# Two stages re-ordered: gathered rows turned inside the second product, and an attention stage with its sums at the head of the step

## The chip, the cores and the metric

The kernel runs on one core of a Trainium2 chip. A core has TensorE (PE in the profile, its weight loads PEld), VectorE (DVE), ScalarE (ACT), GpSimd (POOL) and SyncE (SP), which here only issues transfers. The metric is device time in microseconds (us) of one execution; the median of three runs of the kernel before is 3226.8 us.

## The reference

The input x has 8 sequences of 512 tokens with 256 features. Six residual stages follow each other, each on a layer norm of x:

```python
x = x + 0.5 * L0_ffn(ln(x))    # 64 experts, top 3, capacity 128
x = x + L0_attn(ln(x))
x = x + 0.5 * L0_ffn(ln(x))
x = x + 0.5 * L1_ffn(ln(x))    # 8 experts, top 2, dense
x = x + L1_attn(ln(x))
x = x + 0.5 * L1_ffn(ln(x))
```

The change touches the first two kinds. `L0_ffn` gathers 128 rows for each expert, and computes `gelu(buf @ w1 + b1) @ w2 + b2` (256 to 1024 to 256), scales by the gate and adds the rows back. `L0_attn` is a windowed attention, 16 heads of 16, where each token looks at itself and 31 before it:

```python
strain = disp_win - disp[:, :, :, None, :]
state = masked mean of (strain @ w_state + b_state) over the window
bond_act = gelu(strain @ w_strain + b_strain + state @ w_state_i + state_win @ w_state_j + rel_emb @ w_pos)
damage_act = gelu(strain @ w_damage + b_damage)
logits = bond_act @ w_bond_out + b_bond_out - 10 * sigmoid(damage_act @ w_damage_out + b_damage_out)
out = softmax(masked logits) applied to val_win, then @ w_cproj + b_cproj
```

## The kernel before, in words

The whole of x stays in SBUF (`core.tile`). The stages run one after another, each in a block of its own, in which every engine has a program of its own, written out in order; semaphores join them. An engine that waits holds back all that stands behind it. All of the products named here are in float32, which TensorE does in two passes.

**Sparse stage** (`experts`, twice). Per expert e TensorE runs `up(e + 1)`, `turn_rows(e + 2)`, `down(e)`. `turn_rows` (L1621) transposes the 128 gathered rows in two pieces into one PSUM bank, which VectorE copies to `rows_t` (L1686); `up` (L1633) is the first product, 16 matmuls; `down` (L1644) is the second, 8 matmuls, which accumulate in another bank. GpSimd adds expert e's result back to memory (L1593), for which it waits until the one before has landed, then gathers the rows of expert e + 4 (L1583), all with four buffers. SyncE loads the 2 MB of weights of expert e + 4 when expert e is done.

**First attention** (`attn0_phase`, once). The work of one sequence (a batch) is 16 steps of four relative places for eight heads. In step s:

- GpSimd writes damage chunk s + 1 (L2041), VectorE bond chunk s + 1 (L2373), each into a ring of three buffers;
- ScalarE applies GELU to bond and damage chunk s (L2304, L2309), and after every fourth step a tanh to the group's damage sums (L2317);
- TensorE reduces both chunks of step s - 1 with `columns` (L2088), at the end of its step. Before it in the step stand the other pieces: turning a group's logits, the finishing of one tile of the previous batch's output, spread over four steps (`turn_weights`, `sums`, `turn_ctx`, `project`), and the token products of the next chunks: `make_q`, `make_a`, `make_c`, `values`, tokens and means. The constants `A1_Q, C1_Q, Q1_Q, V_Q, XN_Q, XM_Q, Q0_Q, A0_Q, C0_Q` say in which of the 16 steps each stands.

When a batch's logits are complete, VectorE finds the top of each row (`find_top`, L2407), GpSimd subtracts it (`less_top`, L2048), ScalarE takes exponentials (L2323), and SyncE stores the weights in memory in slanted rows of 128 bytes (`skew_weights`, four stores and one load for a batch), which gives them back shifted to the window. Tile m starts its finishing at step 13 + 4 (m + 4), and waits for the addition of tile m - 1. After the last chunk (step 128) seven tiles, 25 to 31, are left. `softmax_batch` has no upper bound, so a ninth softmax runs in these steps, on data that nobody reads.

## Time and profile before

| | |
|---|---|
| runs | 3226.8, 3223.7, 3229.19 us |
| profiled execution | 3219.98 us, span 3218.2 us |
| busy share of the span | PE 90%, DVE 51%, ACT 47%, POOL 42% |
| mean granted TensorE clock | 0.947 |
| sparse stages, steady part | 159.31 to 612.58 and 1535.97 to 1990.11 us |
| first attention, first to last GELU | 684.65 to 1313.9 us |
| its tail | to 1398.8 us |

The page's busy shares are averages over six stages. Which engine is full in one stage, and which waits, has to be read from windows of that stage. In a row of the timeline the bracket at the end is the idle time of that engine ahead of the row and what ended it. The transfers are issued by SyncE's queue (SPq); the length of such a row is that of the issue, not of the transfer.

### The profile page before, as it was taken

The page shows a single profiled execution, that of the slowest core. Times are in us where ns is not written, and L with a number is a line of the kernel's source. Part 1 is how long each engine was busy: PE and PEld are TensorE (multiplying, and loading weights), DVE is VectorE, ACT ScalarE, POOL GpSimd, SP SyncE. Part 2 cuts the span into 40 slices and gives each one's busy share as a digit, 9 for nine tenths or more (in the row PEclk, how much of TensorE's full clock was granted, in tenths as well). Part 3 has the DMA queues.
Part 4 walks back from the last instruction along what each step waited for, and adds up shares of the span by engine and source line. Part 5 has one row for each costly group of instructions (what it writes and reads, how often), then busy time and mean ns, then how long its engine had stood idle before and what let it go on. Part 6 is the DMA issues. An engine that isn't in the chain of part 4 may idle for free. (4 is left out here: it accounts for less than half of the span.)

```text
span 3218.2 us, 53908 instructions
## 1 busy us (share of the span) xinstructions
PE 2896.9 (90%) x19497; PEld 2067.5 (64%) x19497; DVE 1649.1 (51%) x4513; ACT 1527.6 (47%) x2577; POOL 1346.6 (42%) x1333
## 2 busy tenths in 40 slices
PE   5899999768999999568999999899969999998999
PEld 4799999733444443247999998566635666655666
DVE  4411111168888888455111111566676666665666
ACT  1133333249988888410333332233347777772332
POOL 3444444359989888335344443000043344320000
PEclk9899999989999999757999999899989999998999
DMA  7199999713544444641899997200052233301000
GB/s 278 40 302 317 321 316 319 239 30 20 61 60 60 59 59 60 94 168 53 262 319 321 322 313 236 82 0 0 8 142 72 70 88 95 95 2 37 13 13 20
DMA packets 354987, 431.81 MB, mean 134 GB/s; under 512 B 84528, under 2 KB 312771, under 8 KB 350659
## 3 DMA queue, kind: packets, MB, share of 16 engines
q1 hardware_dynamic: 330178, 395.16, 44.2%
q0 software_dynamic: 24576, 33.57, 4.8%
q8 instruction: 144, 2.36, 0.3%
q14 instruction: 89, 0.72, 0.1%
HBM read 355.80 MB, written 72.88 MB: 133 GB/s over the span
## 5 line engine op out<-in xcount | busy, mean ns | idle before, releaser
L1674 ACT ACTIVATE f_h_t<-f_h_ps,f_b_t 128x128 f32<-128x128 f32 x1024 | 320.4, 364 | 617.1 <-PE f_h_ps L1633 617.1
L2041 POOL TENSOR_TENSOR a_dmg_buf<-a_c 128x2048 f32<-128x2048 f32 x128 | 520.1, 4096 | 65.6 <-PE a_dmg_ps L2088 43.9
L1633 PEld LDWEIGHTS f_h_ps<-f_rows_t,f_w 128*128 128x128 f32 x4096 | 481.5, 193 | 9.9 <-issue 3.5
L1633 PE MATMUL f_h_ps<-f_rows_t,f_w 128*128 128x128 f32 x4096 | 482.6, 276 | 2.3 <-DVE f_rows_t L1686 1.2
L1644 PE MATMUL f_y_ps<-f_w,f_h_t 128*128 128x256 f32 x2048 | 462.9, 379 | 0.0
L1593 POOL DMA_INDIRECT acc_rows<-f_y,f_give x128 | 205.0, 1602 | 509.1 <-DMA acc_rows<-f_y,f_give 372.1
L1644 PEld LDWEIGHTS f_y_ps<-f_w,f_h_t 128*128 128x128 f32 x2048 | 379.3, 190 | 46.4
L2373 DVE SCALAR_TENSOR_TENSOR a_bond_buf<-a_a,a_small_rep,a_q_ps 128x512 f32<-128x512 f32 x512 | 346.9, 741 | 36.8 <-PE a_bond_ps L2088 35.1
L428 DVE SCALAR_TENSOR_TENSOR x_resid<-f_y_ps,f_gate,x_resid 128x256 f32 x512 | 218.7, 479 | 162.5 <-PE f_y_ps L311 156.9
L885 ACT ACTIVATE a_prob<-a_prob,a_neg_top 128x384 f32<-128x384 f32 (+3 forms) x512 | 276.5, 570 | 47.3 <-POOL a_neg_top L702 46.9
L299 PE MATMUL f_h_ps<-f_xn_t,f_w 128*128 128x512 f32 x584 | 282.5, 611 | 3.3 <-DVE f_xn_t L176 1.8
L998 DVE CUSTOM_DVE_ANT_0 a_prob<-a_s_ps,a_factor 128x384 f32<-128x384 f32 (+3 forms) x512 | 234.4, 486 | 86.5 <-PE a_s_ps L779 84.5
L360 ACT ACTIVATE f_h_t<-f_h_ps,f_b 128x512 f32<-128x512 f32 x146 | 100.3, 687 | 368.6 <-PE f_h_ps L299 368.3
L311 PEld LDWEIGHTS f_y_ps<-f_w,f_h_t 128*128 128x128 f32 x1152 | 219.6, 191 | 86.2 <-issue 55.1
L311 PE MATMUL f_y_ps<-f_w,f_h_t 128*128 128x256 f32 x1152 | 270.5, 380 | 0.1
L1686 DVE COPY f_rows_t<-f_t_ps 128x256 f32<-128x256 f32 x128 | 54.4, 425 | 408.4 <-PE f_t_ps L1621 408.4
L2309 ACT ACTIVATE a_dmg_buf<-a_dmg_buf,a_small_rep 128x2048 f32<-128x2048 f32 x128 | 255.2, 1994 | 4.9 <-POOL a_dmg_buf L2041 4.8
L2304 ACT ACTIVATE a_bond_buf<-a_bond_buf,a_bond_act_b 128x2048 f32<-128x2048 f32 x128 | 255.5, 1996 | 2.0 <-DVE a_bond_buf L2373 1.8
L1693 DVE TENSOR_TENSOR f_y_biased<-f_y_ps,f_b 128x256 f32<-128x256 f32 x128 | 54.4, 425 | 393.4 <-PE f_y_ps L1644 381.3
L790 PE MATMUL a_t_ps<-ident,a_prob 128*128 128x128 f32 x1280 | 231.1, 280 | 17.6 <-ACT a_prob_t L896 13.5
L896 ACT COPY a_prob_t<-a_t_ps 128x512 f32<-128x512 f32 (+1 forms) x352 | 192.8, 548 | 100.7 <-PE a_t_ps L790 99.5
L702 POOL TENSOR_SCALAR a_neg_top<-a_top 128x1 f32<-128x1 f32 x512 | 105.1, 209 | 323.5 <-DVE a_top L998 298.5
(333 smaller groups left out, 4274.5 us busy)
## 6 DMA issues: line engine op xcount, KB each, us to landing
f_w<-in_L_ffn_w_dram SPq DMA_DIRECT2D x256, 1024.0 KB
a_skewed<-skew SPq DMA_DIRECT2D x8, 2048.0 KB, 8.4
a_k_s<-parts SPq DMA_DIRECT2D x16, 768.0 KB, 7.8
acc_rows<-x_resid SPq DMA_DIRECT2D x17, 512.0 KB, 4.5
xn_rows<-f_xn SPq DMA_DIRECT2D x16, 512.0 KB, 3.0
x_resid<-acc_rows SPq DMA_DIRECT2D x16, 512.0 KB, 7.5
a_vals<-val_rows SPq DMA_DIRECT2D x64, 128.0 KB, 5.3
skew<-a_bond SPq DMA_DIRECT2D x32, 256.0 KB
```

The lines of the kernel that those rows point to most:

```text
L299: last = nc.tensor.matmul(h_ps[(k * NE + n) % 2][:, :], w1_sb[:, RUN[n], c, :], norm.xn_t[k][:, c, :], start=c == 0, stop=c == DC - 1)
L311: last = nc.tensor.matmul(y_ps[m % YB][:, j, :], h[:, t * P:(t + 1) * P], w2_sb[:, RUN[n], :], start=True, stop=True)
L790: last = nc.tensor.transpose(t_ps[pack % TB][:, col + kb * P:col + (kb + 1) * P], prob[:, u % PR, kb * P:(kb + 1) * P], core.ident[:, :])
L885: nc.scalar.activation(prob[:, u % PR, 0:width], prob[:, u % PR, 0:width], ACT.Exp, bias=neg_top[:, u % PR:u % PR + 1]).then_inc(exp_ready, 1)
L998: nc.vector.tensor_tensor_reduce(out=prob[:, u % PR, 0:width], in0=s_ps[use % SB][:, 0:width], in1=factor[:, S - width:S], scale=1.0, scal ...
L1633: last = nc.tensor.matmul(h_ps[n // HB][:, (n % HB) * P:(n % HB + 1) * P], w1_sb[s][:, c, n * P:(n + 1) * P], rows_t[e % 2][:, c, :], star ...
L1644: last = nc.tensor.matmul(y_ps[k][:, 0:D], h_t[k][:, n, :], w2_sb[e % R][:, n, :], start=n == 0, stop=n == HC - 1)
L1674: nc.scalar.activation(h_t[k][:, n, :], h_ps[n // HB][:, (n % HB) * P:(n % HB + 1) * P], ACT.Gelu, bias=b1_t[:, n, e:e + 1]).then_inc(gelu ...
L2041: nc.gpsimd.tensor_tensor(dmg_buf[n % RING][:, :, :], places(c_sb[h], first_place(dg)), c_sb[h][:, PAD:].unsqueeze(1).broadcast_to([P, DG, ...
L2304: nc.scalar.activation(buf[:, :, :], buf[:, :, :], ACT.Gelu, bias=bond_act_b[:, h:h + 1]).then_inc(bond_act, 1)
L2309: nc.scalar.activation(buf[:, :, :], buf[:, :, :], ACT.Gelu, bias=small_rep[:, B_DAMAGE:B_DAMAGE + 1]).then_inc(dmg_act, 1)
L2373: last = nc.vector.scalar_tensor_tensor(out=bond_buf[n % RING][:, dd, :], in0=a_sb[h][:, d + 1:d + 1 + S], scalar=small_rep[:, POS + d:POS ...
```

## The change

- `down` turns the rows of expert e + 2 between its fourth and its fifth matmul.
- In the attention stage TensorE's step starts with `columns`. `make_q` and `make_a` are cut into a beginning and an end, in two steps, and the constants spread the pieces over the batch. VectorE copies what step s - 1 made at the head of step s, right behind its chunk.
- The first normalisation is VectorE's instead of GpSimd's; the later ones stand one chunk earlier.
- The bias of the output projection is split into three bf16 rows, so its product is one bf16 matmul instead of two float32 passes.
- The stores and loads of the weights go by tile, sixteen and four of them instead of four and one. For the last batch top, subtraction and exponential go by tile too.
- From tile 26 on (`LATE`) tiles start two steps apart and use banks that are free by then, so that they overlap.
- The ninth softmax is gone.

```diff
                 for n in range(HC):
+                    if n == HC // 2 and e + 2 < E:
+                        turn_rows(e + 2)
                     pe.wait_ge(gelu_done, e * HC + n + 1)
                     last = nc.tensor.matmul(y_ps[k][:, 0:D], h_t[k][:, n, :], w2_sb[e % R][:, n, :],
                                             start=n == 0, stop=n == HC - 1)
...
             for e in range(E):
                 if e + 1 < E:
                     up(e + 1)
-                if e + 2 < E:
-                    turn_rows(e + 2)
                 down(e)
 
         @block.scalar
...
-    LAST = CHUNKS + FIRST + TPB * FIN
+    LATE = FINISHES - TPB - 2
+    LATE_FIN = 2
     NTP = 8
     XN, XM, A0, C0, A1, C1 = 0, 2, 4, 5, 6, 7
-    V_Q = (3, 7)
-    XN_Q, XM_Q, Q0_Q, A0_Q, C0_Q = 7, 9, 11, 12, 13
-    A1_Q, C1_Q, Q1_Q = 1, 2, 3
...
+        second = lambda m: dmg_ps if m >= LATE else o_ps
+        ctx_bank = lambda m: bond_ps[1][:, 0:D] if m >= LATE else o_ps[:, D:2 * D]
+        project_bank = lambda m: bond_ps[0] if m >= LATE else o_ps
...
+        def begin(m):
+            return FIRST + (m + TPB) * FIN if m <= LATE else begin(LATE) + (m - LATE) * LATE_FIN
+        FINISH_AT = {begin(m): m for m in range(FINISHES)}
+        LAST = begin(FINISHES - 1) + FIN
...
-            x, now = divmod(s - FIRST, FIN)
-            return x - TPB if s >= FIRST and now == stage else None
...
-            return i - 1 if now == q and i > 0 else None
+            return i - 1 if now == q and 0 < i <= B else None
+        def soft_parts(j):
+            return [slice(x, x + 1) for x in range(TPB)] if j == B - 1 else [slice(0, TPB)]
...
-                sp.wait_ge(exp_done, j + 1)
-                if j:
-                    sp.wait_ge(skew_loaded, j * 16)
-                for a in range(BPT):
-                    row = TPB * NH * SPAN
-                    rows = bass.AP(tensor=skew_dram.tensor, offset=a * WIN * row + 1,
-                                   ap=[[row + 1, WIN], [SPAN, TPB * NH], [1, WIN]])
-                    sp.dma_start(rows, bond[j % 2][a * WIN:(a + 1) * WIN, :, :, :].rearrange(
-                        "p j h w -> p (j h) w")).then_inc(skew_stored, 16)
-                if j:
-                    sp.wait_ge(w_turned, j * TPB)
-                sp.wait_ge(skew_stored, (j + 1) * 16 * BPT)
-                sp.dma_start(skewed[:, :, :].rearrange("p j s -> p (j s)"), skew_dram).then_inc(skew_loaded, 16)
+                row = TPB * NH * SPAN
+                for x in range(TPB):
+                    if x < len(soft_parts(j)):
+                        sp.wait_ge(exp_done, j + x + 1)
+                    if j:
+                        sp.wait_ge(skew_loaded[x], j * 16)
+                    for a in range(BPT):
+                        rows = bass.AP(tensor=skew_dram.tensor, offset=a * WIN * row + x * NH * SPAN + 1,
+                                       ap=[[row + 1, WIN], [SPAN, NH], [1, WIN]])
+                        sp.dma_start(rows, bond[j % 2][a * WIN:(a + 1) * WIN, x, :, :]).then_inc(skew_stored[x], 16)
+                for x in range(TPB):
+                    if j:
+                        sp.wait_ge(w_turned, (j - 1) * TPB + x + 1)
+                    sp.wait_ge(skew_stored[x], (j + 1) * 16 * BPT)
+                    sp.dma_start(skewed[:, x, :], skew_dram[:, x * NH * SPAN:(x + 1) * NH * SPAN]
...
-            normalise(0)
+                for n, tiles in enumerate(soft_parts(j)):
+                    count = tiles.stop - tiles.start
+                    rows = bond[j % 2][:, tiles, :, :].rearrange("p j h w -> p (j h) w")
+                    pool.wait_ge(top_ready, j + n + 1)
+                    nc.gpsimd.tensor_tensor(rows, rows, top[:, tiles.start * NH:tiles.stop * NH, :].broadcast_to([P, count * NH, WIN]),
+                                            ALU.subtract).then_inc(soft_ready, 1)
...
 
             def turn_weights(m):
                 j, x = divmod(m, TPB)
-                if x == 0:
-                    pe.wait_ge(skew_loaded, (j + 1) * 16)
-                before = values_before(FIRST + (m + TPB) * FIN)
...
                 if before:
                     pe.wait_ge(val_copied, before)
-                if m:
+                if m > LATE:
+                    pe.wait_ge(w_copied_act, m)
+                    pe.wait_ge(w_copied_dve, m)
+                elif m == LATE:
+                    pe.wait_ge(tanh_done, ALL_GROUPS)
...
                     pe.wait_ge(proj_added, m)
                 for hp in range(HP):
...
+                if m == LATE:
+                    pe.wait_ge(proj_added, m)
+                if m > LATE:
+                    pe.wait_ge(ctx_ready, m)
...
             def turn_ctx(m):
                 pe.wait_ge(ctx_ready, m + 1)
+                if m == LATE:
+                    pe.wait_ge(logits_copied, ALL_GROUPS)
...
+                if m == 0:
+                    pe.wait_ge(b_out_split, 1)
+                if m > LATE:
+                    pe.wait_ge(proj_added, m)
                 for c in range(DC):
-                    nc.tensor.matmul(o_ps[:, 0:D], ctx_t[:, c, :], w_out_sb[:, c, :], start=c == 0, stop=False)
...
+                    nc.tensor.matmul(project_bank(m)[:, 0:D], ctx_t[:, c, :], w_out_sb[:, c, :], start=c == 0, stop=False)
+                nc.tensor.matmul(project_bank(m)[:, 0:D], ones[:, :], b_out_rows[:, :], start=False, stop=True).then_inc(proj_ready, 1)
 
             def turn_tokens(i, c):
...
-            def make_q(i, h):
+            def begin_q(i, h):
                 if i:
                     pe.wait_ge(bond_pre, (i - 1) * STEPS + (h + 1) * NQ)
                 pe.wait_ge(tok_copied, i * NTP + XM + DC)
                 for c in range(DC):
                     nc.tensor.matmul(q_ps[h][:, :], token_w[:, c, h, TO_Q, :], xn_t[i % NX][:, c, PAD:],
                                      start=c == 0, stop=False)
+            def end_q(i, h):
...
+                if 0 < s <= CHUNKS:
+                    columns(s - 1, 0)
+                    columns(s - 1, 1)
...
+                if i < B:
+                    if q == A1_Q:
+                        begin_a(i, 1)
+                    if q == A1_Q + 1:
+                        end_a(i, 1)
...
-                    if q == Q0_Q:
-                        make_q(i + 1, 0)
                     if q == A0_Q:
-                        make_a(i + 1, 0)
+                        begin_a(i + 1, 0)
+                    if q == A0_Q + 1:
+                        end_a(i + 1, 0)
                     if q == C0_Q:
                         make_c(i + 1, 0)
-                if 0 < s <= CHUNKS:
-                    columns(s - 1, 0)
-                    columns(s - 1, 1)
+                    if q == Q0_Q:
+                        begin_q(i + 1, 0)
+                    if q == Q0_Q + 1:
+                        end_q(i + 1, 0)
+                if i < B and q in V_Q:
+                    values(s, i, V_Q.index(q))
...
 
-                act.wait_ge(soft_ready, j + 1)
-                nc.scalar.activation(bond[j % 2][:, :, :, :], bond[j % 2][:, :, :, :], ACT.Exp).then_inc(exp_done, 1)
+                for n, tiles in enumerate(soft_parts(j)):
+                    act.wait_ge(soft_ready, j + n + 1)
+                    nc.scalar.activation(bond[j % 2][:, tiles, :, :], bond[j % 2][:, tiles, :, :], ACT.Exp).then_inc(exp_done, 1)
 
...
-            inverse_std(0, 1, 1)
+            dve.wait_ge(std_ready, 1)
+            nc.vector.reciprocal(rstd[:, 0:TPB], std[:, 0:TPB])
+            nc.vector.drain()
+            for j in range(TPB):
+                last = nc.vector.tensor_scalar(xn[:, j, :], core.tile(1, j), mean_var[:, j, 0:1], rstd[:, j:j + 1],
+                                               ALU.subtract, ALU.mult)
+            last.then_inc(xn_ready, 1)
...
             for s in range(LAST):
-                i, q = divmod(s, STEPS)
+                if s == 4:
+                    inverse_std(1, B, 2)
                 if s + 1 < CHUNKS:
...
+                    if i + 1 < B:
+                        if q in (XN_Q, XN_Q + 1):
+                            copy_tokens(i + 1, q - XN_Q)
+                        if q in (XM_Q, XM_Q + 1):
+                            copy_means(i + 1, q - XM_Q)
+                        if q == A0_Q + 1:
+                            copy_a(i + 1, 0)
+                        if q == C0_Q:
+                            copy_c(i + 1, 0)
+                    if q in V_Q:
+                        copy_values(i, V_Q.index(q))
                 m = finishing(s, 0)
                 if is_tile(m):
```

What the lists of instructions show (f_0 is the first sparse stage, a_1 the attention stage). First TensorE in the sparse stage, for the expert whose second product reads `w_0`, the lines of before and of the change:

```order
-L1621 MATMUL f_0_t_ps<-ident,f_0_rows 128x128 x2
-L1644 MATMUL f_0_y_ps<-f_0_w_0,f_0_h_t 128x256 x8
+L1647 MATMUL f_0_y_ps<-f_0_w_0,f_0_h_t 128x256 x4
+L1621 MATMUL f_0_t_ps<-ident,f_0_rows 128x128 x2
+L1647 MATMUL f_0_y_ps<-f_0_w_0,f_0_h_t 128x256 x4
```

The two transposes stand four matmuls later; nothing else moves on TensorE there.

TensorE in batch 2 of the attention stage, steps 11 and 12, before. `q_ps` and `tok_ps` with `token_w` are the token products, L2156 and L2157 the projection:

```order
L2149 MATMUL a_1_o_ps<-ident,a_1_ctx 128x128 x2
L2184 MATMUL a_1_q_ps<-a_1_xn_t,a_1_token_w 128x512 x2
L2187 MATMUL a_1_q_ps<-a_1_xm_t,a_1_token_w 128x512 x2
L2088 MATMUL a_1_bond_ps<-a_1_bond_buf,a_1_col_bond 32x512 x4
L2088 MATMUL a_1_dmg_ps<-a_1_dmg_buf,a_1_col_damage 32x512 x4
L2156 MATMUL a_1_o_ps<-a_1_w_out,a_1_ctx_t 128x256 x2
L2157 MATMUL a_1_o_ps<-a_1_b_out,a_1_ones 128x256
L2194 MATMUL a_1_tok_ps<-a_1_xn_t,a_1_token_w 128x512 x2
L2197 MATMUL a_1_tok_ps<-a_1_xm_t,a_1_token_w 128x512 x2
L2088 MATMUL a_1_bond_ps<-a_1_bond_buf,a_1_col_bond 32x512 x4
L2088 MATMUL a_1_dmg_ps<-a_1_dmg_buf,a_1_col_damage 32x512 x4
```

The same steps in the change, and the sums at the head of step 13:

```order
L2117 MATMUL a_1_bond_ps<-a_1_bond_buf,a_1_col_bond 32x512 x4
L2117 MATMUL a_1_dmg_ps<-a_1_dmg_buf,a_1_col_damage 32x512 x4
L2189 MATMUL a_1_o_ps<-ident,a_1_ctx 128x128 x2
L2246 MATMUL a_1_tok_ps<-a_1_xm_t,a_1_token_w 128x512 x2
L2117 MATMUL a_1_bond_ps<-a_1_bond_buf,a_1_col_bond 32x512 x4
L2117 MATMUL a_1_dmg_ps<-a_1_dmg_buf,a_1_col_damage 32x512 x4
L2200 MATMUL a_1_o_ps<-a_1_w_out,a_1_ctx_t 128x256 x2
L2201 MATMUL a_1_o_ps<-a_1_b_out_rows,a_1_ones 128x256
L2253 MATMUL a_1_tok_ps<-a_1_xn_t,a_1_token_w 128x512 x2
L2117 MATMUL a_1_bond_ps<-a_1_bond_buf,a_1_col_bond 32x512 x4
L2117 MATMUL a_1_dmg_ps<-a_1_dmg_buf,a_1_col_damage 32x512 x4
```

Before, a whole q product, and then a projection and a whole a product, stand between two column sums; now half an a product (L2246), and then a projection and a c product (L2253).

TensorE's last tiles, before (`skewed` is the load that tile waits for):

```order
L2111 MATMUL a_1_t_ps<-ident,a_1_skewed 128x128 x4
L2111 MATMUL a_1_o_ps<-ident,a_1_skewed 128x128 x4
L2122 MATMUL a_1_o_ps<-a_1_vals,a_1_turned 32x32 x32
L2149 MATMUL a_1_o_ps<-ident,a_1_ctx 128x128 x2
L2156 MATMUL a_1_o_ps<-a_1_w_out,a_1_ctx_t 128x256 x2
L2157 MATMUL a_1_o_ps<-a_1_b_out,a_1_ones 128x256
L2111 MATMUL a_1_t_ps<-ident,a_1_skewed 128x128 x4
L2111 MATMUL a_1_o_ps<-ident,a_1_skewed 128x128 x4
L2122 MATMUL a_1_o_ps<-a_1_vals,a_1_turned 32x32 x32
L2149 MATMUL a_1_o_ps<-ident,a_1_ctx 128x128 x2
L2156 MATMUL a_1_o_ps<-a_1_w_out,a_1_ctx_t 128x256 x2
L2157 MATMUL a_1_o_ps<-a_1_b_out,a_1_ones 128x256
```

And in the change:

```order
L2143 MATMUL a_1_t_ps<-ident,a_1_skewed 128x128 x4
L2143 MATMUL a_1_dmg_ps<-ident,a_1_skewed 128x128 x4
L2189 MATMUL a_1_bond_ps<-ident,a_1_ctx 128x128 x2
L2158 MATMUL a_1_o_ps<-a_1_vals,a_1_turned 32x32 x32
L2200 MATMUL a_1_bond_ps<-a_1_w_out,a_1_ctx_t 128x256 x2
L2201 MATMUL a_1_bond_ps<-a_1_b_out_rows,a_1_ones 128x256
L2143 MATMUL a_1_t_ps<-ident,a_1_skewed 128x128 x4
L2143 MATMUL a_1_dmg_ps<-ident,a_1_skewed 128x128 x4
L2189 MATMUL a_1_bond_ps<-ident,a_1_ctx 128x128 x2
L2158 MATMUL a_1_o_ps<-a_1_vals,a_1_turned 32x32 x32
L2200 MATMUL a_1_bond_ps<-a_1_w_out,a_1_ctx_t 128x256 x2
L2201 MATMUL a_1_bond_ps<-a_1_b_out_rows,a_1_ones 128x256
```

A tile's transposes now stand ahead of the context and the projection of the tile before it, in banks of their own.

## Rows read from the trace of the kernel before

**Rows 1.** Windows, steady sparse stage: us, busy us by engine, clock, DMA.
```profile
159.31:612.58 453.27, 447.71 (x3053) 417.66 (x3051) 73.36 (x183) 152.76 (x488) 192.25 (x180) 1.00 0.99 314
604.00:605.00 1.00, 1.00 (x12) 1.00 (x10) 0.00 (x0) 0.73 (x4) 0.00 (x0) 1.00 0.42 119
```

**Rows 2.** Timeline, TensorE, one expert step: start us, us, engine, line, operation.
```profile
300.39 0.38 PE L1621 MATMUL f_t_ps<-ident,f_rows 128*128 128x128 f32 x2
300.61 3.62 PE L1644 MATMUL f_y_ps<-f_w,f_h_t 128*128 128x256 f32 x16
304.06 3.73 PE L1633 MATMUL f_h_ps<-f_rows_t,f_w 128*128 128x128 f32 x32
307.63 0.38 PE L1621 MATMUL f_t_ps<-ident,f_rows 128*128 128x128 f32 x2
```

**Rows 3.** The transposes of gathered rows (L1621), what ended their waits: us, times.
```profile
  DMA f_rows<-xn_rows,f_take: 37.3, 69
```

**Rows 4.** The same windows view, first attention: batches 0, 1, 2, 6, 7, tail.
```profile
682.00:758.60 76.60, 63.31 (x352) 22.20 (x352) 69.53 (x149) 67.14 (x39) 72.82 (x21) 0.91 0.05 14
758.60:832.20 73.60, 63.00 (x436) 24.81 (x436) 60.40 (x92) 68.78 (x41) 73.53 (x22) 0.98 0.52 62
832.20:913.97 81.77, 75.01 (x685) 33.93 (x684) 66.50 (x106) 69.84 (x45) 73.49 (x22) 0.96 0.48 59
1159.25:1239.72 80.47, 73.72 (x685) 33.44 (x685) 66.51 (x106) 69.68 (x45) 73.42 (x22) 0.98 0.49 60
1239.72:1313.90 74.18, 63.18 (x638) 25.79 (x637) 59.00 (x94) 69.61 (x44) 64.81 (x17) 0.95 0.52 65
1313.90:1398.80 84.90, 46.44 (x576) 29.56 (x572) 25.01 (x37) 9.69 (x12) 7.28 (x2) 0.56 0.44 47
```

**Rows 5.** Timeline, TensorE, between two column sums of batch 4.
```profile
1058.00 1.13 PE L2156 MATMUL a_o_ps<-a_w_out,a_ctx_t 128*128 128x256 f32 x4
1059.06 0.69 PE L2157 MATMUL a_o_ps<-a_b_out,a_ones 1*128 1x256 f32 x2
1059.68 1.98 PE L2194 MATMUL a_tok_ps<-a_xn_t,a_token_w 128*128 128x512 f32 x4
1063.31 1.06 PE L2088 MATMUL a_bond_ps<-a_bond_buf,a_col_bond 128*32 128x512 f32 x8
```

**Rows 6.** Timeline, ScalarE, tanh and its waits in one batch.
```profile
1020.48 0.69 ACT L2317 ACTIVATE a_tanh<-a_dmg_ps,a_damage_b 128x512 f32<-128x512 f32 x1 [4.52 <-PE a_dmg_ps L2088]
1065.31 0.69 ACT L2317 ACTIVATE a_tanh<-a_dmg_ps,a_damage_b 128x512 f32<-128x512 f32 x1 [6.35 <-PE a_dmg_ps L2088]
```

**Rows 7.** Timeline, GpSimd, two chunks.
```profile
1004.55 4.60 POOL L2041 TENSOR_TENSOR a_dmg_buf<-a_c 128x2048 f32<-128x2048 f32 x1 [0.32 <-PE a_dmg_ps L2088]
1065.35 3.71 POOL L2041 TENSOR_TENSOR a_dmg_buf<-a_c 128x2048 f32<-128x2048 f32 x1 [3.41 <-PE a_dmg_ps L2088]
```

**Rows 8.** Timeline of the tail: SyncE's queue, TensorE, VectorE.
```profile
1328.43 10.17 SPq L1955 DMA_DIRECT2D skew<-a_bond  x4
1350.81 0.34 SPq L1960 DMA_DIRECT2D a_skewed<-skew  x1
1359.23 1.11 PE L2111 MATMUL a_t_ps<-ident,a_skewed 128*128 128x128 f32 x4 [14.81 <-DMA a_skewed<-skew]
1398.33 0.42 DVE L2455 TENSOR_TENSOR x_resid<-a_o_ps,x_resid 128x256 f32<-128x256 f32 x1 [3.32 <-PE a_o_ps L2157]
```

**Rows 9.** Timeline, TensorE, first transposes of the attention stage.
```profile
656.27 1.11 PE L2165 MATMUL a_tok_ps<-ident,a_xn 128*128 128x128 f32 x4 [4.91 <-POOL a_xn L2030]
```

**Rows 10.** Groups by line, softmax steps: busy us, mean ns, idle before.
```profile
L2407 DVE TENSOR_REDUCE a_top<-a_bond 128x64 f32<-128x2048 f32 x9 | 20.6, 2286 | 0.8
L2048 POOL TENSOR_TENSOR a_bond<-a_bond,a_top 128x2048 f32<-128x2048 f32 x9 | 32.8, 3648 | 68.7 <-DVE a_top L2407 68.7
L2323 ACT ACTIVATE a_bond<-a_bond 128x2048 f32<-128x2048 f32 x9 | 17.2, 1910 | 17.7 <-POOL a_bond L2048 17.6
```

**Rows 11.** Timeline, SyncE's queue, a 256 KB load in long rows.
```profile
647.72 0.42 SPq L1937 DMA_DIRECT2D a_dmg_buf<-in_L_attn_w_disp_dram  x1
```

123 lines of the change are left out of this document (71 added, 52 removed).

## The prediction

> **What bounds the kernel now.** I read the windows by stage first, then the waits and the timeline inside the two stages that the change touches. The kernel runs six stages one after another, so each is judged by itself. Nothing in the dense and second-attention code changes, and its time is left as it is.
>
> The sparse stage runs twice. In its steady part (61 expert steps in 453.27 us, 7.43 us each) TensorE is busy 447.71 us at full clock, so TensorE's order is the path [rows 1]. One step without a wait is 7.24 us: two transposes of the gathered rows, eight second-product matmuls (16 passes), then the next first product, back to the transposes [rows 2]. The difference, 0.19 us a step, sits in front of the transposes, which waited for the gather in 69 records, 37.3 us in all for both queues of TensorE and both stages, the start-up waits included, so about half a microsecond each [rows 3]. The DMA engines are nearly as full: share 0.99 at 314 GB/s, but with lulls, such as one microsecond at 0.42 and 119 GB/s [rows 1].
>
> The first attention stage pipelines 128 chunks of 16 per batch: GpSimd and VectorE write a chunk each, ScalarE applies two GELUs, TensorE reduces them to columns. Batch 1 takes 73.60 us, in which GpSimd works 73.53: there GpSimd bounds [rows 4]. Batches 2 to 6 take 81.77 to 80.47 us (407.5 us together) with GpSimd still at 73.4 to 73.5, and TensorE at 73.7 to 75.0 [rows 4]. What differs is that TensorE now also turns and multiplies the previous batch's weights. Its work is not too much but lumped: a projection (1.68 us) and a whole `make_a` (3.63 us) stand between two column sums, 5.31 us in one piece [rows 5]. ScalarE's tanh then waits 6.35 us for the sums and at the other lump 4.52 [rows 6], and GpSimd waits 3.41 us for its buffer [rows 7].
>
> The tail after the last GELU is 84.9 us at mean clock 0.56, so near the lower level of 1.2 GHz [rows 4]. From the first store of the last weights (1328.43) to the load's issue (1350.81) go 22.38 us, to the first turn 8.42 more, and from there to the end of the last addition (1398.33 + 0.42) 39.5 us for four tiles, strictly one behind the other [rows 8].
>
> **The change part by part.** *Sparse stage.* The transposes move from ahead of the second product into its middle: same instructions, 3.45 / 2 = 1.73 us later [rows 2]. The excess of a step was 0.19 us on average and a recorded wait 0.54 (37.3 / 69) [rows 3], so 1.73 us more should cover nearly all of them. What is late next: the copy of the turned rows on VectorE must end before the next first product, 1.7 us after the turn, and nothing else is queued on VectorE then. Bounds per stage: 453.27 - 61 x 7.24 = 11.6 us if all goes; nothing if the DMA engines are the limit and the slack is used up once. The second stage is like the first, so 0 to 24 us. I take 20, since the lulls show that DMA has something to spare.
>
> *Start of attention.* The first normalisation moves from GpSimd to VectorE, before the wait for the small weights; TensorE waited 4.91 us for it [rows 9]. The next thing needed is VectorE's own small matrices, so I take 3.8 of 4.91 (bounds 2 and 4.9).
>
> *Middle.* Column sums of a step now come first and the other work after them; each 3.63 us product of q and a is cut in two, over two steps, and projections, values and means are spread. The heaviest step after its sums holds a projection and a half product (or a c product, which is as long): 1.06 + 0.1 to 0.6 + 1.8 = some 3.0 to 3.5 us against 5.31 [rows 5]. The bias product of a projection becomes one bf16 pass instead of two float32 ones of 0.62 us together: I take 0.5 us saved, four times a batch. So tanh should hardly wait, and GpSimd's 73.5 us of work is the floor, which batch 1 shows to be attainable. I don't expect the floor: after the stretch in which GpSimd subtracts the top and normalises, TensorE has 75.0 - 2 = 73 us of work in the same batch, all but equal, ScalarE 69.8, and a ring of three buffers does not hide every difference. Both ends are 73.5 and 81.5; I take 76.5, nearer to batch 1. Five batches: 407.5 - 382.5 = 25 us. Batch 0 (76.60 us, GpSimd busy 72.82) can give 3, batch 7 (74.18 us, GpSimd 64.81, ScalarE 69.61) 2.5 [rows 4].
>
> A new wait comes with it: the sums stand at the head of TensorE's step, so a late GELU holds back all that is behind, the token products for the next batch among them. The first q product now ends at step 14, and VectorE's chunk 16 needs it at once. That is in the 76.5.
>
> *Tail.* Top, subtraction, exponential, store and load go by tile, so the first store starts when a quarter of them is done. Top, subtraction and exponential take 2.29 + 3.65 + 1.91 us for a batch [rows 10]; three quarters of that, 5.9 us, fall out, and I take 5.5 for the waits between. All sixteen stores are issued before the first load, and they are the same 1 MB in the same pieces, so I leave 22.4 us for them; the first of four loads then needs a quarter of 8.42 and its latency, some 3 us. The first turn comes 5.5 + 5.4 = 11 us earlier. From there the tiles overlap, and TensorE's own work at the low clock decides: it was busy 46.44 us in the tail for seven tiles and the last column sums, some 6.3 us a tile [rows 4]. Four tiles, the projection of tile 27, which now stands behind the wait (2 us), and 2 us of copies to the end are 29.5 instead of 39.5. Together 21 us (bounds 12, if the stores cost more, and 32, if the clock is high). The ninth, unused softmax (the page counts nine of each step for eight batches) goes as well; it is in these numbers.
>
> If every store and load were bound by its own fixed cost, the tile split would be a loss. By the trace, a DMA of 256 KB in long rows takes 0.42 us to issue and a store of 256 KB in 128-byte rows 2.54 [rows 8, 11], so the cost is in the pieces, whose number stays. The Trainium skill, DMA: Bandwidth & Descriptors, section Rules for kernel authors, says to coalesce small transfers, as one under 64 KB pays mostly overhead; the stores become just 64 KB. By its Anatomy of one DMA a transfer has about 2 us of fixed cost: one after the other, sixteen would take an estimated 32 us and the tail would gain nothing. The rival below is what that would do.
>
> **Sum.** 20 + 3.8 + 3 + 25 + 2.5 + 21 = 75.3 us. The profiled execution took 3219.98 us, so 3144.7 for one like it; the median of the runs is 3226.8, 6.8 above, and the forecast for it is 3151.
>
> **The rivals.** *DMA takes it back.* With TensorE's wait gone the step asks for 3% more from engines at share 0.99; the gathers come later until the wait is back at its new place. For it: the share, and each scatter waits for the one before to land. Against: the lulls. The sparse stages give 4 instead of 20: 3167.
>
> *The middle stays.* GpSimd's chunk takes 3.71 us when VectorE is quiet and up to 4.60 beside it [rows 7]. If the tighter schedule makes 4.6 the rule, 16 chunks cost 8 us more a batch, and GpSimd is at 81.5. Or the head-of-step sums hold the token products back so that the wait only moves. Then batches give 3 or 4 us in all instead of 30.5: 3178. The Trainium skill, GPSIMD Engine Reference, section 1. Specifications, states that GpSimd shares its SBUF interfaces with VectorE and contends with some of its instructions. The trace agrees in that the same instruction varies so; but the overlapped VectorE work is the same amount as before, and batch 1 ran to 73.6 with it.
>
> *Slower: the stores' issue.* If a store of 64 KB costs SyncE the same 2.54 us as one of 256 KB, sixteen take 40.6 us; with 12.2 us from last issue to landing and 8.4 for the load that is 61 us, where half a batch (41 us, steps 5 to 13) is available [rows 8, 4]. Each of seven batches would be 20 us late, the tail 30: about 3350. It decides from some 1.55 us a store, where the loss eats all gains (7 x (16 x 1.55 - 20.4) + 16 x 1.55 - 10.2 is the 45 us of the sparse stages, start and tail). Against: the long-row DMA's 0.42 us [rows 11].
>
> **How the numbers follow.** Forecast (all parts pay, 3120 to 3165 by itself) 0.60; DMA takes it back 0.16; the middle stays 0.15; the stores 0.05; 0.04 for changes that cancel within 0.2%, about what a measurement of this kernel can tell from no change. The first three are all faster by over 0.2% (6.5 us): 0.91, within 0.03, slower 0.06. The range goes from all upper bounds at nearly once (3118) to both faster rivals together (3151 + 16 + 27 = 3194, taken as 3192).
>
> **What would show it.** Sparse: transposes without a DMA wait and a step of 7.24 to 7.30 us; a step still at 7.4 speaks for the DMA rival. Middle: ScalarE's tanh waits under 1 us, batches 2 to 6 at 75 to 78 us, GpSimd above 0.94 busy; chunks of 4.6 us or token copies waiting on TensorE speak for the second. Tail: first turn some 35 us after the last GELU, instead of 45.3, and under 7 us between tiles. SyncE's issue of sixteen stores near 10 us; 40 us would prove me wrong in sign.

## The result, and the profile after

The changed kernel takes 3188.84 us (median of 4 runs) against 3225.25 for the one before on the same chip: ratio 0.9893, 95% interval 0.9875 to 0.9911, so 36 us faster, with 29 to 40 in the interval. The forecast was 75 faster; the time lies inside the stated range, at its upper end, with less than half of the gain. The profiled execution has a span of 3189.3 us, 28.9 under that of before. The table takes both spans apart (starts and ends of the first and last instruction of each part):

| part | before | after | difference | forecast |
|---|---|---|---|---|
| sparse stages, first product to last | 478.5 + 478.4 | 470.3 + 469.6 | -17.0 | -20 |
| attention, start to first GELU | 43.3 | 45.4 | +2.1 | -3.8 |
| batch 0 | 73.97 | 88.94 | +15.0 | -3 |
| batch 1 | 73.58 | 72.54 | -1.0 | 0 |
| batches 2 to 6 | 407.5 | 402.4 | -5.1 | -25 |
| batch 7 | 74.18 | 76.39 | +2.2 | -2.5 |
| tail, to the last addition | 84.9 | 58.7 | -26.2 | -21 |
| all else | | | +1.0 | 0 |

Batch 0 is counted here from ScalarE's table load ahead of the first GELU (684.65 before), and in [rows 4] from 682.00, so it has 73.97 us where the forecast read 76.60. These are single executions: the attention stage of the same code differs by up to 19 us between two of them (experiment 1), so only the large terms can be told one by one. The two ends of the sum, sparse stages and tail, came about as forecast, and everything between them did not.

**Sparse stage.** The window of 61 steps (columns as in [rows 1]), what ended the transposes' waits, and one step of TensorE:

```profile
161.47:606.51 445.04, 442.88 (x3051) 413.56 (x3050) 75.34 (x183) 152.30 (x488) 193.44 (x181) 1.00 1.00 319
```
```profile
  DMA f_rows<-xn_rows,f_take: 16.5, 15
```
```profile
304.69 1.89 PE L1647 MATMUL f_y_ps<-f_w,f_h_t 128*128 128x256 f32 x8
306.42 0.38 PE L1621 MATMUL f_t_ps<-ident,f_rows 128*128 128x128 f32 x2
```

A step is 445.04 / 61 = 7.30 us where it was 7.43 [rows 1]; the waits for gathered rows fell from 37.3 us in 69 records [rows 3] to 16.5 in 15, the start-up ones among them. The transposes now stand between two halves of the second product.

**Attention by windows**, batches 0, 1, 2, 7 and tail, against [rows 4]:

```profile
678.57:767.51 88.94, 60.51 (x337) 22.15 (x338) 82.03 (x148) 66.82 (x40) 70.63 (x21) 0.83 0.00 1
767.51:840.05 72.54, 64.34 (x439) 23.56 (x438) 60.59 (x92) 68.54 (x41) 72.54 (x22) 0.95 0.57 66
840.05:920.67 80.62, 74.08 (x682) 32.16 (x681) 66.37 (x106) 70.39 (x44) 75.75 (x23) 0.96 0.51 60
1242.44:1318.83 76.39, 63.90 (x638) 24.91 (x636) 60.58 (x97) 70.13 (x43) 63.25 (x16) 0.96 0.53 63
1318.83:1377.60 58.77, 32.12 (x575) 22.72 (x570) 19.99 (x39) 8.48 (x14) 4.06 (x4) 0.74 0.66 81
```

Batch 0 shows VectorE 82.03 us busy, where it was 66.9 before. In batches 2 to 6 TensorE's busy time fell by 0.5 us on average (74.54 to 74.03) and the length by 1.0; TensorE is still idle some 6.5 us in each. GpSimd's chunks last 4.09 us on average in these batches, before and after. The tail is not only shorter: its mean clock is 0.74, from 0.56.

**Batch 0: seven small instructions.** VectorE's rows, then GpSimd's chunks at the same time:

```profile
709.70 2.46 DVE L2524 CAST a_b_out_part<-a_b_out 3x256 bf16<-3x256 f32 x1
712.23 4.17 DVE L2526 TENSOR_TENSOR a_b_out_rest<-a_b_out,a_b_out_part 3x256 f32<-3x256 f32 x1
716.33 4.58 DVE L2527 TENSOR_SCALAR a_b_out_sum<-a_b_out_part,ident 3x256 f32<-3x256 bf16 x1
720.99 3.74 DVE L2529 CAST a_b_out_part<-a_b_out_rest 3x256 bf16<-3x256 f32 x1
```
```profile
708.28 3.73 POOL L2069 TENSOR_TENSOR a_dmg_buf<-a_c 128x2048 f32<-128x2048 f32 x1
711.95 4.17 POOL L2069 TENSOR_TENSOR a_dmg_buf<-a_c 128x2048 f32<-128x2048 f32 x1
716.08 4.69 POOL L2069 TENSOR_TENSOR a_dmg_buf<-a_c 128x2048 f32<-128x2048 f32 x1
720.73 3.85 POOL L2069 TENSOR_TENSOR a_dmg_buf<-a_c 128x2048 f32<-128x2048 f32 x1
```

These four of the seven instructions that split the projection's bias handle 3 x 256 elements and last 2.46 to 4.58 us. They end at 712.16, 716.40, 720.91 and 724.73; GpSimd's four chunks end at 712.01, 716.12, 720.77 and 724.58. Each of the four ends 0.14 to 0.28 us behind a GpSimd instruction; the other three take 0.41 to 0.47 us each, when GpSimd has stopped. VectorE's next bond chunk stands behind all seven and starts at 726.09; batch 0 is 15 us longer.

**Middle.** TensorE between two column sums, as [rows 5]; ScalarE's tanh, as [rows 6]:

```profile
1004.24 1.13 PE L2200 MATMUL a_o_ps<-a_w_out,a_ctx_t 128*128 128x256 f32 x4
1005.30 0.28 PE L2201 MATMUL a_o_ps<-a_b_out_rows,a_ones 3*128 3x256 bf16 x1
1005.51 1.98 PE L2241 MATMUL a_tok_ps<-a_xn_t,a_token_w 128*128 128x512 f32 x4
1007.42 1.07 PE L2117 MATMUL a_bond_ps<-a_bond_buf,a_col_bond 128*32 128x512 f32 x8
```
```profile
1005.10 0.67 ACT L2377 ACTIVATE a_tanh<-a_dmg_ps,a_damage_b 128x512 f32<-128x512 f32 x1
```

The forecast lump of 3 to 3.5 us is 3.2 (1004.24 to 1007.42), from 5.31, and the tanh has no wait in front of it. What is new stands before GpSimd's subtraction of the top, and behind it on TensorE. First the kernel before, batch 5: GpSimd's subtraction, the tanh ahead of the exponential, and TensorE's wait for the copy behind the exponential.

```profile
1096.69 3.64 POOL L2048 TENSOR_TENSOR a_bond<-a_bond,a_top 128x2048 f32<-128x2048 f32 x1 [0.89 <-DVE a_top L2407]
```
```profile
1102.37 0.69 ACT L2317 ACTIVATE a_tanh<-a_dmg_ps,a_damage_b 128x512 f32<-128x512 f32 x1 [4.53 <-PE a_dmg_ps L2088]
```
```profile
1110.59 1.08 PE L2122 MATMUL a_o_ps<-a_vals,a_turned 128*32 128x32 f32 x64 [4.45 <-ACT a_turned L2329]
```

Then the change, batch 4:

```profile
1021.89 3.65 POOL L2078 TENSOR_TENSOR a_bond<-a_bond,a_top 128x2048 f32<-128x2048 f32 x1 [3.48 <-DVE a_top L2470]
```
```profile
1031.34 1.06 PE L2117 MATMUL a_dmg_ps<-a_dmg_buf,a_col_damage 128*32 128x512 f32 x8 [1.68 <-ACT a_dmg_buf L2369]
...
1035.04 1.06 PE L2158 MATMUL a_o_ps<-a_vals,a_turned 128*32 128x32 f32 x64 [2.04 <-ACT a_turned L2390]
...
1038.35 1.94 PE L2117 MATMUL a_bond_ps<-a_bond_buf,a_col_bond 128*32 128x512 f32 x8 [1.21 <-ACT a_bond_buf L2364]
```

GpSimd sits idle 3.48 us for VectorE's top; before, that wait was 0.9. TensorE then waits 1.68, 2.04 and 1.21 us in one stretch around the exponential, where it waited 4.45 us at once before. Over batches 2 to 6 TensorE's idle time that ended with ScalarE went from 4.45 us a batch to 5.48, and what ended with VectorE from 2.51 to 0.96.

**Start.** GpSimd's memset, two of VectorE's copies beside it, and TensorE's products of the token weights:

```profile
643.27 3.50 POOL L2087 MEMSET a_vals<- 128x4096 f32 x1
```
```profile
644.50 2.30 DVE L2601 COPY a_b_state<-a_small_rep 128x2 f32<-128x2 f32 x1
644.57 2.23 DVE L2540 COPY a_xn_t<-a_tok_ps 128x512 f32<-128x512 f32 x1
```
```profile
650.27 3.78 PE L2283 MATMUL a_q_ps<-a_inner,a_dmg_buf 128*128 128x512 f32 x4 [0.58 <-DVE a_inner L2612]
```

TensorE no longer waits for the normalisation [rows 9], but the copies take 2.2 to 2.3 us beside the memset (0.15 and 0.69 before), and the four products, 1.98 us before, take 3.78, so they run at the lower of the clock's two levels. In this trace the granted clock rises 23.1 us after the stage's start (633.16 to 656.25), behind these products; before, 17.8 us after it (641.35 to 659.16), ahead of them. This does not go with the code alone: of the thirteen traces with the new start twelve have 3.71 to 3.78 us and one 3.38 (experiment 6, both helpers moved), and of the three with the start of before two have 1.98 and one 3.44 (sums first alone).

**Tail**, as [rows 8]: SyncE's stores and loads, the first transposes of each tile, the last addition.

```profile
1329.97 18.57 SPq L1983 DMA_DIRECT2D skew<-a_bond  x16
1348.64 8.25 SPq L1988 DMA_DIRECT2D a_skewed<-skew  x4
```
```profile
1357.16 1.11 PE L2143 MATMUL a_t_ps<-ident,a_skewed 128*128 128x128 f32 x4 [15.82 <-DMA a_skewed<-skew]
1363.13 0.66 PE L2143 MATMUL a_t_ps<-ident,a_skewed 128*128 128x128 f32 x4
1367.02 0.66 PE L2143 MATMUL a_t_ps<-ident,a_skewed 128*128 128x128 f32 x4
1370.90 0.66 PE L2143 MATMUL a_t_ps<-ident,a_skewed 128*128 128x128 f32 x4
```
```profile
1377.11 0.42 DVE L2519 TENSOR_TENSOR x_resid<-a_bond_ps,x_resid 128x256 f32<-128x256 f32 x1 [1.43 <-PE a_bond_ps L2201]
```

The sixteen stores take 18.57 us to issue, 1.16 each on average, where four took 10.17. Single ones differ much: the first seven take 0.33 to 0.51 us, the later ones up to 3.54. From the first store to the first load go 18.7 us (22.4 before), to the first turn 8.5 more (8.4), though this load brings only a quarter of what the one before did. The first turn comes 38.3 us after the last GELU instead of 45.3, and the tiles then follow 3.9 us apart at full clock.

### The profile page after: what moved, and what is told of

The parts are those of the page before. It is cut to its first block and busy times, and to the rows that moved or that the text cites. A ratio compares the mean times of both kernels' runs of the same rounds, so it can differ in the third digit from the quotient of the medians.

```text
span 3189.3 us, 54032 instructions
## 1 busy us (share of the span) xinstructions
PE 2881.4 (90%) x19465; PEld 2047.0 (64%) x19465; DVE 1665.2 (52%) x4524; ACT 1528.2 (48%) x2579; POOL 1339.6 (42%) x1331
## 5 line engine op out<-in xcount | busy, mean ns | idle before, releaser
L1647 PE MATMUL f_y_ps<-f_w,f_h_t 128*128 128x256 f32 x2048 | 483.5, 379 | 0.0
L1647 PEld LDWEIGHTS f_y_ps<-f_w,f_h_t 128*128 128x128 f32 x2048 | 369.9, 190 | 39.9
L311 PEld LDWEIGHTS f_y_ps<-f_w,f_h_t 128*128 128x128 f32 x1152 | 219.6, 191 | 87.6 <-issue 55.5
L311 PE MATMUL f_y_ps<-f_w,f_h_t 128*128 128x256 f32 x1152 | 270.8, 380 | 1.9 <-ACT f_h_t L360 1.9
L790 PEld LDWEIGHTS a_t_ps<-ident,a_prob 128*128 128x128 f32 x1280 | 145.9, 142 | 110.8 <-issue 49.6
```

Source lines behind the costliest of these rows:

```text
L311: last = nc.tensor.matmul(y_ps[m % YB][:, j, :], h[:, t * P:(t + 1) * P], w2_sb[:, RUN[n], :], start=True, stop=True)
L790: last = nc.tensor.transpose(t_ps[pack % TB][:, col + kb * P:col + (kb + 1) * P], prob[:, u % PR, kb * P:(kb + 1) * P], core.ident[:, :])
L1647: last = nc.tensor.matmul(y_ps[k][:, 0:D], h_t[k][:, n, :], w2_sb[e % R][:, n, :], start=n == 0, stop=n == HC - 1)
```

## The experiments

All medians are against runs of the kernel before on the same chip; "the early split" is the first kernel of experiment 2, on which the later ones build. The same code differs by up to 1.7 us a batch from one execution to another, so batch lengths are given as means over batches 2 to 6, and totals as ratios.

**1. The sparse edit alone, and the change without it.**

```diff
 for n in range(HC):
+    if n == HC // 2 and e + 2 < E:
+        turn_rows(e + 2)
...
-                if e + 2 < E:
-                    turn_rows(e + 2)
                 down(e)
```

> Only the sparse edit on the kernel before. In the two profiles the stage from its first product to its last second product fell by 8.2 and 8.8 us. If the parts don't depend on each other, this kernel is 17 us faster than before (ratio 0.9947, about 3208 us), with the steps at 7.24 to 7.30 us and the waits for gathered rows under 20 us. Rival: part of the whole's gain from the sparse stages is drift between two executions; then the gain is under 10 us (ratio over 0.997).

> The change without its sparse edit. By the two profiles the attention stage with its start and tail gives 12 us (start +2, batch 0 +15, batch 1 -1, batches 2 to 6 -5, batch 7 +2, tail -26), so about 3213 us, ratio 0.996, with batch 0 at 89 us and batches 2 to 6 at 80.5. If the stages interact (the attention stage's start depends on how the sparse stage leaves the clock), the start differs from 45.4 us by over 2.

Alone: ratio 0.9934 (0.9915 to 0.9952), 3210.74 us. Without it: 0.9948 (0.9929 to 0.9967), 3216.53 us. The product of the two is 0.9882, the whole change 0.9893, so no dependence between the stages shows beyond the intervals. In the profile of the sparse edit alone both stages are 11 to 12 us shorter, and its attention stage, whose code is that of before, is 19 us longer than in the profile of before: such is the spread of one execution. The change without the sparse edit starts its attention stage in 45.6 us, as the whole change does, with batch 0 at 88.95; its batches 2 to 6 take 81.48 us, not the 80.5 that was expected. In the sparse edit alone, with the code of before, they take 82.37. So the fall from 81.50 to 80.48 in the two main profiles is no more than two executions of the same code differ by.

**2. The split of the bias moved, and taken out.**

```diff
             nc.vector.drain().then_inc(biases_ready, 1)
+            split_bias()
             copy_a(0, 0)
...
-                if s == 5:
-                    split_bias()
```

> The change, with the splitting of the projection's bias (seven small VectorE instructions) moved from step 5 of batch 0 to ahead of the first a copy, where VectorE idles 8.96 us and GpSimd does nothing. Theory: each of these small instructions waited for the end of a GpSimd instruction (2.46 to 4.58 us for 3x256 elements), 16.3 us in all. Then they take under 0.5 us each here, under 5 us in all, hidden; batch 0 falls from 88.9 to 73 us, and the kernel is 15 to 16 us faster than the changed one, about 3173 us (ratio to before 0.984). Rival: the small instructions are slow by themselves (three rows, drains between); then they take 16 us here too, the start grows by 7 us, and the total falls by 8 or 9.

> The change with the projection's bias as before: one float32 row in two passes, no splitting. Batch 0 falls to 73 us as in the kernel with the early split. Theory that TensorE's work sets batches 2 to 6 outside the softmax stretch: they grow by the four bias products, 4 x 0.2 to 0.35 us, to 81.3 to 82 us each (from 80.5), and the kernel is 4 to 7 us slower than the one with the early split, about 3178. Rival, GpSimd sets them: they stay at 80.5 us, and the total equals that of the early split within 2 us.

The early split: ratio 0.9833 (0.9812 to 0.9853), 3179.34 us. Three of its seven instructions, and batch 0:

```profile
660.44 0.28 DVE L2524 CAST a_b_out_part<-a_b_out 3x256 bf16<-3x256 f32 x1
660.79 0.41 DVE L2526 TENSOR_TENSOR a_b_out_rest<-a_b_out,a_b_out_part 3x256 f32<-3x256 f32 x1
661.54 0.28 DVE L2529 CAST a_b_out_part<-a_b_out_rest 3x256 bf16<-3x256 f32 x1
```
```profile
677.12:750.54 73.42, 58.02 (x337) 20.43 (x338) 65.92 (x141) 66.71 (x39) 70.39 (x21) 0.91 0.00 1
```

The same instructions take 0.28 to 0.41 us where GpSimd does nothing, all seven 2.8 us, and batch 0 is 73.42 us. Their own size is not the cost; the first theory is confirmed and its rival out. The Trainium skill, SBUF — State Buffer, section SBUF: two separate sides, says that VectorE and GpSimd share a pair of ports: whichever instruction starts first holds it to its end and the other one waits, if VectorE's runs in a mode that uses both ports, or has two inputs in SBUF while GpSimd's reads SBUF. By that rule a small instruction should end right behind a GpSimd instruction, and the trace agrees (0.14 to 0.28 us behind). That the ports are what holds them up is the page's account; the runs show that GpSimd's work beside them does.

With the bias in float32 and no split the ratio is 0.9859 (0.9835 to 0.9882), 3183.66 us. Its batches 2 to 6 take 82.1 us on average. TensorE works 76.3 us a batch there, 2.3 more; one of the five batches, 84.55 us long, has a lower clock (0.94, the others 0.96), and the other four, 81.3 to 81.7 us, lie at the early split's upper end. The intervals overlap, so this pair doesn't tell the bias product's worth in the total. It does show why TensorE's busy time hardly fell: with the bias as before it is 76.3 us where it was 74.5, so the rest of the change adds about as much as the bias product saves, in part through the clock (0.954 on average against 0.966).

**3. TensorE's work, GpSimd's two helpers, the place of the sums.** Each is the early split with one edit: the q products' second half left out; `normalise` three chunks earlier; `less_top` a chunk later; the sums at the end.

```diff
 # normalise apart
-                if q == 4 and i + 1 < B:
+                if q == (1 if i else 4) and i + 1 < B:
                     normalise(i + 1)
...
 # top later (GpSimd)
-                j = softmax_batch(s, 3)
+                j = softmax_batch(s, 4)
                 if j is not None:
                     less_top(j)
```

> The early split, and the q products' second half (the means' part) left out: TensorE has 3.76 us less to do in each batch, everything else is as in the early split. Batches 2 to 6 there take 81.2 us with TensorE busy 74.2. Theory that TensorE's work sets the pace outside the softmax stretch: they fall by 3 to 3.8 us each, to about 77.8, and the total by 18 to 25. Rival, the pace is set by GpSimd (73.5 busy, and 3.2 us in which it waits for the top): under 1 us a batch, total within 6 us of the early split.

> The early split, and GpSimd's normalisation (4.8 us) for the next batch moved from right behind the subtraction of the top (3.65 us) to three chunks earlier, so that GpSimd is away from its chunks for at most 4.8 us at once instead of 8.5. In the changed kernel ScalarE then waits 2.8 us for the damage chunk once a batch. If the burst of two helpers in a row costs the batch, batches 2 to 6 fall by 2 to 3 us (to 78.5 to 79), total 12 to 18 us; if GpSimd's sum alone counts or TensorE sets the pace, they stay within 1 us and the total within 5 us.

> The early split, and GpSimd subtracts the top one chunk later, so that it doesn't stand idle for VectorE's top (3.2 us a batch). Theory that GpSimd's idle time for the top is on the path: batches 2 to 6 fall by 2 to 3.2 us each. Rival: the exponential, and with it ScalarE's table loads, comes later by a chunk's 4 us and TensorE waits for the copy behind it: the batches stay or grow by up to 2 us.

> The early split, and the column sums back at the end of TensorE's step, all else (the halved products, the constants, the tail) kept. If the position of the sums is worth what the forecast gave it, batches 2 to 6 grow by 2 us or more each (total +10 or more) and tanh waits for the sums again. If only the amount of work counts, they stay within 1 us, and the total within 5 us.

In the table the rest is the length less TensorE's busy time, so its idle time.

| kernel | ratio (95%) | batches 2 to 6, mean us | TensorE busy | rest |
|---|---|---|---|---|
| before | 1 | 81.50 | 74.54 | 6.96 |
| the change | 0.9893 (0.9875 to 0.9911) | 80.48 | 74.03 | 6.45 |
| early split | 0.9833 (0.9812 to 0.9853) | 81.19 | 74.06 | 7.13 |
| less TensorE work | 0.9802 (0.9786 to 0.9818) | 78.34 | 71.25 | 7.09 |
| normalise apart | 0.9855 (0.9835 to 0.9875) | 80.71 | 73.80 | 6.91 |
| top later | 0.9787 (0.9770 to 0.9803) | 78.05 | 74.05 | 4.00 |
| sums last | 1.0040 (1.0026 to 1.0055) | 88.78 | 76.72 | 12.06 |
| sums first alone (below) | 1.0082 (1.0067 to 1.0098) | 85.09 | 75.78 | 9.31 |

Windows of one batch: less TensorE work, top later, sums last.

```profile
894.08:972.37 78.29, 71.48 (x676) 31.22 (x672) 66.24 (x106) 70.25 (x44) 73.25 (x22) 0.93 0.53 62
```
```profile
976.23:1053.94 77.71, 74.23 (x682) 32.64 (x681) 66.38 (x106) 70.26 (x44) 73.45 (x22) 0.96 0.50 62
```
```profile
930.71:1019.50 88.79, 76.76 (x684) 33.84 (x680) 66.63 (x105) 70.32 (x44) 73.51 (x22) 0.94 0.47 54
```

Less work on TensorE passes through in full: busy time and length both fall by 2.8 us, the rest stays at 7.1, so the first theory holds in kind and GpSimd's 73.5 us is not what sets these batches. Its sizes are missed: the batches fell by 2.8 us and not by 3 to 3.8, and the total by 10 us by the ratios, by 16 over the eight batches of the two profiles, where 18 to 25 was expected. TensorE's 3.76 us of products gave 2.8 of its busy time, as the mean granted clock of these batches fell too, from 0.962 to 0.943. The normalisation's place is worth nothing that can be told, although GpSimd has no wait for the top in batches 2 to 6 there either. So GpSimd's idle time is not by itself what costs: there the normalisation fills it, and the next damage chunk starts as late as in the change, 24.2 us into the batch. With the later subtraction a damage chunk fills it. GpSimd goes from chunk to subtraction without idling, TensorE's idle time that ends with ScalarE falls from 5.3 to 3.3 us a batch, and in the batch shown its waits shrink to two.

```profile
997.01 3.65 POOL L2078 TENSOR_TENSOR a_bond<-a_bond,a_top 128x2048 f32<-128x2048 f32 x1
```
```profile
1007.05 0.76 PE L2158 MATMUL a_o_ps<-a_vals,a_turned 128*32 128x32 f32 x64 [1.01 <-ACT a_turned L2390]
...
1010.37 1.94 PE L2117 MATMUL a_bond_ps<-a_bond_buf,a_col_bond 128*32 128x512 f32 x8 [1.94 <-ACT a_bond_buf L2364]
```

Two more kernels with the same middle (memset late in experiment 4, tiles apart in 5) have 79.1 and 79.8 us, so the subtraction's place is worth 1.4 to 3.1 us a batch by single executions, and 0.46% of the whole by the two ratios, 15 us. With the sums last the changed kernel is slower than the one before. The waits of the tanh are back there, 14.4 us a batch (10.7 to 11.9 before), and GpSimd's wait for the top is down to 0.1. TensorE's idle time that ends with ScalarE is 4.2 us a batch (5.3 in the early split); what has grown, from 1.8 us to 7.8, is what ends with VectorE: TensorE's next piece for the tokens needs a copy that VectorE has not made yet.

**4. The remaining idle time, and the start.** ScalarE copies the turned weights before the exponential; the values' first product a step earlier besides (`V_Q = (6, 15)`); the 3.5 us memset held back; each on the kernel with the later top.

```diff
 # memset late (GpSimd)
+            pool.wait_ge(biases_ready, 1)
             nc.gpsimd.memset(vals[:, :, :, :], 0.0).then_inc(pads_ready, 1)
```

> The kernel whose top is subtracted a chunk later (ratio 0.9787), and ScalarE copies the turned weights before the exponential instead of behind it. TensorE there waits 1.0 us a batch for that copy and 1.9 to 2.0 for the bond chunk after the table loads. Theory that a batch is TensorE's busy time plus its idle time around the exponential (74.1 + 4.0 us): the first wait goes, the second stays or takes a part of it back, so batches 2 to 6 fall by 0 to 1 us, total 0 to 7 us (ratio 0.977 to 0.979). Rival, that second wait grows by as much: exactly nothing.

> As the one with the copy first, and the first half of the values' product (1.5 to 1.9 us of TensorE) one step earlier, from behind the wait after the table loads to ahead of it. Theory that TensorE's idle time there is on the path and other work can fill it: batches 2 to 6 fall by a further 1.0 to 1.9 us, to 76 to 76.5 us, total 6 to 13 us below the kernel with the copy first. Rival, the stretch is bound by ScalarE's chunks and tables and not by what TensorE does in it: within 0.5 us a batch.

> The kernel whose top is subtracted a chunk later, with GpSimd's 3.5 us memset of the value blocks held back until VectorE's start-up copies are done. Theory: those copies (2.30, 2.23, 1.63 and 0.90 us in the changed kernel, 0.15 to 0.69 alone) waited for the end of the memset. Then they take 0.15 to 0.7 us here, TensorE's second turn of the tokens no longer waits 0.64 to 0.99 us, and the start is 1.5 to 2.5 us shorter than 44.9 to 46.4, unless TensorE's clock takes it back. Total: 0 to 3 us, which the runs may not tell.

Copy first: 0.9798 (0.9776 to 0.9819), batches of 79.28 us, within the spread of the kernels with the same middle (78.1 to 79.8). The rival was right: the first wait went, and the second grew from 1.96 to 3.05 us. Values early: 0.9818 (0.9793 to 0.9843), 79.38 us. Neither gained, and the theory that other TensorE work can fill that time falls, for its rival; the ratio of 0.976 to 0.978 that it would have given lies outside the interval. Memset late: 0.9783 (0.9755 to 0.9811), nothing that the total tells, but the rows do:

```profile
638.29 0.15 DVE L2602 COPY a_b_state<-a_small_rep 128x2 f32<-128x2 f32 x1
638.35 0.67 DVE L2541 COPY a_xn_t<-a_tok_ps 128x512 f32<-128x512 f32 x1
655.37 3.63 DVE L2525 CAST a_b_out_part<-a_b_out 3x256 bf16<-3x256 f32 x1
```

Two copies of the start take 0.15 and 0.67 us again. The memset, now at 655.35 to 658.87, holds up the first instruction of the split instead: 3.63 us, where it took 0.28 in experiment 2. The start stays at 44.9 us all the same; its four products take 3.78 us as before.

**5. The tail's overlap.**

```diff
-    LATE = FINISHES - TPB - 2
+    LATE = FINISHES
...
-            return FIRST + (m + TPB) * FIN if m <= LATE else begin(LATE) + (m - LATE) * LATE_FIN
+            return FIRST + (m + TPB) * FIN
```

> The kernel whose top is subtracted a chunk later, with the last tiles four steps apart and in the banks of all others, so that each waits for the addition of the one before (LATE is never reached); the softmax by tile and the sixteen stores stay. Tiles are 3.9 us apart in the changed kernel (at full clock) and were 9.45 us apart before (at half). If the overlap is worth its waits alone, three intervals grow from 3.9 to 6 to 7 us at full clock: 8 us; if the overlap is also what keeps TensorE's clock up, they grow to 9.5 and the tail by 16 to 20 us (ratio 0.984 to 0.985).

Ratio 0.9850 (0.9827 to 0.9873): 20 us over the kernel with the later top. From the end of the last bond GELU the tail takes 80.0 us, against 61.1 there, and 65.1 and 65.3 in two more kernels whose tail is the same code (memset late, and both helpers moved in experiment 6). The transposes of the second and third of its last four tiles:

```profile
1344.63 1.08 PE L2143 MATMUL a_t_ps<-ident,a_skewed 128*128 128x128 f32 x4 [0.61 <-DVE x_resid L2519]
1353.23 1.08 PE L2143 MATMUL a_t_ps<-ident,a_skewed 128*128 128x128 f32 x4 [0.61 <-DVE x_resid L2519]
```

The tiles are 8.6 us apart at mean clock 0.50, not 3.9. The three distances between the last four tiles sum to 25.8 us, against 13.7 in the change. TensorE is busy 6.11 us of each 8.60 at this clock and 3.27 of 3.89 at full clock, so by that estimate some 8.5 of these 12 us are the clock and the rest are waits. The second theory holds in kind: beside its waits the overlap gives TensorE's higher clock.

**6. The sums first alone, and both of GpSimd's helpers moved.** The first is the kernel before with `columns` at the head of the step and nothing else.

> The kernel before, with the column sums at the head of TensorE's step and nothing else changed: whole q and a products, the constants of before, float32 bias. With the sums last again the changed kernel's batches 2 to 6 grew from 81.2 to 88.8 us, so the position alone could be worth much. If it is, this kernel's batches 2 to 6 fall from 81.8 by 2 us or more (total 10 or more faster, ratio under 0.997) without any halving. If TensorE's busy time and its idle time around the exponential set a batch, they stay within 1.5 us of 81.8, tanh's waits vanish or become waits for the chunk buffers, and the total stays within 8 us (ratio 0.9975 to 1.0025).

> The top subtracted a chunk later (ratio 0.9787), and the normalisation three chunks earlier besides, so that GpSimd's two helpers stand apart and neither waits. Alone, the second edit moved the early split's ratio from 0.9833 to 0.9855, nothing that can be told. If what is left of TensorE's idle time (4.0 us a batch) still comes from GpSimd's 8.5 us away from its chunks, batches 2 to 6 fall by 1 to 2 us and the ratio to 0.976 or 0.977; if it is ScalarE's exponential with its two table loads (4.5 us), they stay within 1 us and the ratio at 0.9775 to 0.980.

The sums first alone: ratio 1.0082, 27 us slower than before. One batch, and GpSimd's subtraction in it:

```profile
1014.98:1100.15 85.17, 75.85 (x688) 33.31 (x684) 66.45 (x106) 70.54 (x43) 73.35 (x22) 0.96 0.50 57
```
```profile
1037.21 3.64 POOL L2048 TENSOR_TENSOR a_bond<-a_bond,a_top 128x2048 f32<-128x2048 f32 x1 [5.89 <-DVE a_top L2407]
```

GpSimd waits 5.89 us for the top in each batch, where it was 0.9 before; neither theory of the expectation named this. The tanh's waits fell to 2.0 us a batch, and TensorE's idle time that ends with ScalarE rose from 4.45 to 8.6. Both helpers moved: 0.9792 (0.9776 to 0.9809), 78.93 us, nothing beyond the later top alone. By its expectation what is left is then ScalarE's exponential with its table loads; no run took that away, so it is argued and not shown.

## Why the prediction was wrong

- **Sparse stage, right.** 17.0 us in the profiles against 20, 7.30 us a step, at the edge of the range named; alone it is worth 0.66%, 21 us. The DMA engines did not take it back.
- **The bias product, a cost put at nothing.** The forecast said "I take 0.5 us saved, four times a batch" and priced what it removes from TensorE; that size was right (2.3 us of busy time a batch in experiment 2). It never priced what it adds to VectorE, seven instructions at step 5 of batch 0, although it named the contention of the two engines for the chunks. They cost 16.4 us there (709.70 to 726.09) and 15.5 of batch 0; experiment 2 shows both. The 3 us that batch 0 was to give had little room either: the window of [rows 4] starts 2.65 us ahead of ScalarE's table load for the first GELU.
- **Batches 2 to 6, the largest miss: 5 us instead of 25.** "So tanh should hardly wait, and GpSimd's 73.5 us of work is the floor": the first half came true, the second does not follow, and it is the step that failed. A batch was, and is, TensorE's busy time (74 to 75 us) plus 6.5 to 7 us in which it stands still, for ScalarE around the exponential (4.45 us before, 5.48 after) and for VectorE's copies and sums (2.51, 0.96). Less TensorE work shortened it (experiment 3), with GpSimd's work as it was. I read the waits of an engine behind a full TensorE, and used batch 1, where TensorE has 11 to 12 us less to do, as proof that GpSimd's floor can be reached. The row of batch 2 had both numbers: 75.01 busy of 81.77. The tanh's waits went, some 11 us a batch, and the length hardly moved; but that they were worth nothing is not shown. One of the four, 4.53 us, stands ahead of the exponential, and from that tanh to the copy for which TensorE then waits 4.45 us ScalarE has no gap (1102.37 to 1110.54), so this one may well feed TensorE's wait. In the change TensorE's wait did fall, to 2.04 us, while 3.4 us of new ones for ScalarE's chunks came beside it. With the subtraction a chunk later besides, a batch takes 78.1 to 79.8 us. No run moves the subtraction in the kernel before alone, so how much of this gain needs the tanh's waits gone stays open.
- **The rival "the middle stays"**, held at 0.15, is what the batches did, but not by its first mechanism: a chunk of GpSimd took 4.09 us on average before and after. Its second, that the sums at the head of the step only move the wait, came nearer; it looked for it at the token products, and it came at the top.
- **The sums at the head of the step.** By itself it loses 3.6 us a batch: the logits are turned behind the sums, the top comes later and GpSimd idles for it (5.9 us alone, 3.5 in the change, 0.9 before, 0.1 with the sums last again). With the new constants it is needed: without it a batch takes 88.8, with 7.8 us in which TensorE waits for VectorE's copies. Neither part gains by itself, and together they come out even.
- **Start.** The wait of 4.9 us went, and the start still took 2.1 us more: 1.3 us through copies beside the memset (from TensorE's first instruction to the token weights' products go 8.0 us, with the memset late 6.7), and at least 1.8 in those products, which run at the lower clock. Why the clock rises later there was not tried. The start varied from 42.6 to 46.7 us over the kernels with all of their work, the code of before with 43.3, 45.2 and 46.7 among them, so no sign is shown for this term, only that 3.8 us did not come.
- **Tail, right in sum, wrong inside.** 26 instead of 21. The stores and load took 27.2 us to the first turn against 25.4 forecast. The term that was off is the load's: it was to need a quarter of 8.42 us and its latency, some 3 us, and the turn came 8.5 us after its issue; the stores, for which 22.4 was left, took 18.7, although a store of a quarter took 1.16 us to issue and not 0.64. The first store came 3.4 us earlier and not 5.5; the tiles took 20.4 instead of 29.5, as the forecast kept the clock of before (0.56). So two errors cancelled, and that the sum came near is in part luck. Batch 7 lost 2.2 us, for which no experiment was made. The rival of the stores' issue would have needed 1.55 us a store. The 2 us of fixed cost that the prediction takes from the Trainium skill (DMA: Bandwidth & Descriptors, Anatomy of one DMA) are stated there for transfers that GpSimd issues, and these are SyncE's; the stores overlapped, with 18.7 us from first store to first load where that estimate has 32.

The forecast's total was within reach: with the split moved and the top subtracted a chunk later, two moved calls, the kernel takes 3153.51 us, ratio 0.9787 (69 us by the ratio), and none of the kernels tried that do all of the work is faster by more than the intervals tell.

## What to carry to other kernels

Ask of each engine's wait who was working meanwhile: the length of a wait of ScalarE behind a full TensorE is no measure of what it is worth (some 11 us a batch went here, and the batch stayed). A stage's length is best tested as the busy time of its fullest engine plus that engine's idle time, named piece by piece; a wait elsewhere counts by what it adds to one of these pieces. Price what an edit adds on every engine, and look what runs beside it: seven tiny instructions cost 16 us in one place and nothing in another. When TensorE's work comes in short pieces between waits, count the clock too, on both sides of the change.

## What the runs showed of the hardware

- VectorE's cast, tensor_tensor and tensor_scalar of 3 x 256 elements take 0.28 to 0.41 us alone, and up to 4.58 us while GpSimd runs tensor_tensor over 128 x 2048; a cast took 3.63 beside a memset. VectorE's scalar_tensor_tensor of 128 x 512, with one input in PSUM, was not held up: in the kernel before its median is 0.742 us with GpSimd working beside it (449 of them) and 0.748 with GpSimd idle (12).
- Sixteen stores of 64 KB in 128-byte rows took SyncE's queue 17.2 to 18.8 us to issue, batch by batch, and four of 256 KB 10.0 to 11.4. Single ones in the tail took 0.33 to 3.54 and 0.32 to 5.11 us, the first of each the shortest.
- In the tail a load of 2 MB in 16 KB rows landed 8.38 us after its issue, and of its quarters in 4 KB rows, issued one by one, three landed after 5.65 to 8.89 us (the first one's landing is not in the trace; the turn that needs it came after 8.5).
- In the tail the same tile takes 3.9 us at full clock and 8.6 at 0.50; which one it is was set by whether tiles overlap.
- In one batch of the kernel with the later top the granted clock fell to the lower level after TensorE had stood still for 1.01 and, with some 1.4 us of work between, for 1.94 us; its next eight sums took 1.94 us instead of 1.06.
